# Stage four's first shifted image copies written by VectorE and ScalarE in place of DMAs, five and two unused products on PE ahead of its convolution, and the later image moments moved into its first pass

## What is computed

```
x = x + _L3_conv_ref(_gn(x), ...)

off = conv2d(x, w_off, b_off, (1, 1), 'SAME')              # 3x3, 32 channels in
off = jnp.tanh(group_norm(off, g_gn_off, b_gn_off, K))
upper = jnp.cumsum(y_off[:, CENTER + 1:], axis=1)          # and lower, from the centre outwards
y_coord = jnp.arange(H)[None, None, :, None] + EXT * y_off_new
deformed = jax.vmap(samp)(x, y0i, y1i, x0i, x1i, wy, wx)   # bilinear, here in y alone
out = conv2d(deformed, w_dsc, b_dsc, (K, 1), 'VALID')
out = group_norm(out, g_gn, b_gn, w_dsc.shape[0] // 4)
return jax.nn.relu(out)
```

## Time and profile before

| | |
|---|---|
| median of 3 runs | 1568.82 us (1565.77 to 1573.45) |
| the profiled execution | 1568.02 us, of which the span is 1566.2 us |
| PE, PEld busy | 1358.1 us (87%), 580.5 us (37%) |
| VectorE busy | 1240.1 us (79%) |
| ScalarE busy | 974.9 us (62%) |
| GpSimd busy | 1044.7 us (67%) |
| granted PE clock, mean | 0.939 of full speed |
| stage three's block | about 1074 to 1272 us of the span |
| stage four's block | about 1272 us to the end |

### The profile page before, as it was taken

One profiled execution on the slowest core, in us unless ns is written; L12 is line 12 of the kernel. 1 busy time (PEld: TensorE's weight loads), 2 busy tenths in 40 slices (PEclk: granted clock), 3 DMA queues, 4 the chain that ended last, 5 costly groups with the idle time before them and its releaser, 6 DMA issues. The chain is left out here.

```text
span 1566.2 us, 34078 instructions
## 1 busy us (share of the span) xinstructions
PE 1358.1 (87%) x11812; PEld 580.5 (37%) x11812; DVE 1240.1 (79%) x5001; ACT 974.9 (62%) x1649; POOL 1044.7 (67%) x773
## 2 busy tenths in 40 slices
PE   5999999999999999999995699994887848676775
PEld 1333333333333333333332466661656611121111
DVE  6899999999999999999997455555222258887886
ACT  2688888888888888888883334431000025766654
POOL 4789999999999999999991033233000029998885
PEclk8699999999999999999998899997999978998977
DMA  7000000000000000000000554321000012202001
GB/s 181 9 2 9 4 9 4 2 9 5 9 4 2 9 4 2 12 2 2 1 2 3 125 122 110 84 51 55 2 2 1 2 46 46 46 1 49 11 14 27
DMA packets 24587, 42.31 MB, mean 27 GB/s; under 512 B 8576, under 2 KB 14208, under 8 KB 24416
## 3 DMA queue, kind: packets, MB, share of 16 engines
q1 hardware_dynamic: 21920, 37.64, 10.0%
q10 hardware_dynamic: 2496, 2.50, 0.7%
HBM read 9.20 MB, written 2.10 MB: 7 GB/s over the span
## 5 line engine op out<-in xcount | busy, mean ns | idle before, releaser
L435 POOL TENSOR_SCALAR l_onehot<-l_ib,c_iota 128x512 bf16<-128x512 f16 x250 | 390.0, 1560 | 48.5 <-ACT l_ib L382 48.5
L545 DVE FIND_INDEX8 l_idx<-l_top,l_scored 128x8 uint32<-128x256 f32 x1024 | 413.1, 419 | 0.0
L240 PE MATMUL ps<-l_ct_slot,l_res 32*128 32x512 f32 x2048 | 409.5, 609 | 0.0
L562 DVE CUSTOM_DVE_ANT_0 l_scored<-ps,l_gain 128x256 f32<-128x256 f32 x1024 | 377.8, 416 | 8.4 <-ACT l_gain L364 7.5
L364 ACT ACTIVATE l_gain<-ps 128x768 f32<-128x768 f32 (+1 forms) x384 | 284.2, 740 | 106.6 <-PE ps L240 103.1
L1702 POOL TENSOR_TENSOR l_isum<-l_term 128x512 f32<-128x512 f32 x160 | 204.6, 1307 | 35.5 <-DVE l_term L1806 21.1
L263 PE MATMUL ps<-l_onehot,l_cbp_slot 128*32 128x512 bf16 x3072 | 213.5, 385 | 4.0 <-ACT l_signed L388 2.6
L234 PE MATMUL ps<-l_csq,l_row_slot 32*128 32x512 bf16 x1024 | 154.7, 394 | 12.9 <-DVE l_top L562 6.2
L240 PEld LDWEIGHTS ps<-l_ct_slot,l_res 32*128 32x128 f32 x2048 | 155.8, 193 | 10.7 <-issue 0.8
L1432 PE MATMUL ps<-l_isum,w_l_w_dsc 64*64 64x512 f32 x640 | 104.4, 714 | 59.7 <-POOL l_isum L1702 58.7
L382 ACT CAST l_ib<-ps 128x512 f16<-128x512 f32 x256 | 149.4, 583 | 2.0 <-PE ps L254 2.0
(11 more groups left out here) (178 smaller groups left out, 1935.7 us busy)
## 6 DMA issues: line engine op xcount, KB each, us to landing
l_xi<-l_xt SPq DMA_DIRECT2D x128, 128.0 KB
l_xi<-l_xz SPq DMA_DIRECT2D x36, 144.2 KB, 3.1
X<-in_x SPq DMA_DIRECT2D x16, 128.0 KB, 8.9
l_xr<-l_xt SPq DMA_DIRECT2D x32, 64.0 KB
out<-X SPq DMA_DIRECT2D x16, 128.0 KB, 2.2
l_ct<-in_codes_t SPq DMA_DIRECT2D x4, 448.0 KB, 15.0
l_ct_slot<-l_ct SPq DMA_DIRECT2D x7, 256.0 KB, 2.2
l_cbp_slot<-l_cbp SPq DMA_DIRECT2D x8, 96.0 KB, 1.9
```

What stands on the lines that cost most here:

```text
L240: pe.matmul(ps[:, at + n - FIRST[k], :], res[rows, i, P * tt:P * (tt + 1)], ct_slot[rows, par, :], start=False, stop=True, skip_group_chec ...
L435: nc.gpsimd.tensor_scalar(onehot[:, i % 2, g, 0, :], ib16[:, i % 2, g, :], iota[:, 0:1], None, ALU.is_equal).then_inc(s_near, 1)
L545: nc.vector.max_index(idx8[:, i % 2, n, :], top[:, i % 2, n:n + 1].to_broadcast([P, 8]), scored[:, WIDE * (k % 3) + n - FIRST[k], :]).then ...
L562: nc.vector.tensor_tensor_reduce(out=scored[:, WIDE * (k % 3) + m, :], in0=ps[:, WIDE * (k % 2) + m, :PAIRED], in1=gain[:, WIDE * (k % 2) ...
```

## The change

For quarter 0 the copies in `xi` are no longer sent from `xz`. `xi` is set to zero by GpSimd as a whole, and twelve pieces (g, kx) of each half image are written straight from X by VectorE (four with kx = 0, two with kx = 1) and ScalarE (four with kx = 2, two with kx = 1), normalised on the way. The upper pieces have 17 rows of 32, the lower 15. ScalarE needs `shift` for it, which VectorE now makes in stage three. `xz` of quarter 0 is no longer written. PE multiplies five times into bank 0 once the first four adds are through, and twice more at the head of stage four; nothing reads these products. The moments of quarter 1 stay at the start of stage four, those of quarters 2 and 3 go behind items 4, 6, 8 and 10 of pass 0, with the aggregation behind item 12, the square root at ScalarE's item 11 of pass 1 and the rest behind VectorE's item 13 of pass 1. Names and loops cut:

```diff
+DIRECT = {"dve": [(g, 0) for g in range(G)] + [(0, 1), (1, 1)], "act": [(g, 2) for g in range(G)] + [(2, 1), (3, 1)]}
+PIECE_ROWS = ((0, H // 2 + 1), (H // 2 + 1, H))
+def shifted(xi, g, kx, piece):
+    first, last = PIECE_ROWS[piece]
+    at = (1 + first) * PADW + 1 - kx
+    return xi[C * kx:C * kx + C, g, at:at + (last - first) * PADW].rearrange("p (y x) -> p y x", x=PADW)[:, :, 0:W]
 block_l2, sync:
-            sp.wait_ge(s_next_xz, START + 1)
-            load_columns(sp, xz, xi, 0, range(0, 2), PIECES[0], s_xi[0])
 block_l2, gpsimd:
             nc.gpsimd.memset(xz[:], 0.0).then_inc(s_zero, 1)
+            nc.gpsimd.memset(xi[:], 0.0).then_inc(s_zero, 1)
 block_l2, tensor, at the end:
+            pe.wait_ge(s_out, START + G)
+            for n in range(5):
+                pe.matmul(ps[:, 0, :], ident[:], wt[:].rearrange("p d k m -> p (d k m)")[:, 0:BANK],
+                          start=True, stop=True)
 block_l2, scalar, at the end:
-            act.wait_ge(s_next_xz, START + 1)
-            load_columns(act, xz, xi, 0, range(2, G), PIECES[0], s_xi[1])
+            act.wait_ge(s_next, START + 5)
+            act.wait_ge(s_zero, START + 2)
+            for g, kx in DIRECT["act"]:
+                rows = slice(C * g, C * g + C)
+                nc.scalar.activation(shifted(xi, g, kx, 0), image_rows(X, g, 0), ACT.Identity, bias=xshift[rows, 0:1],
+                                     scale=xrstd[rows, 0:1]).then_inc(s_xi["act"], 1)
 block_l2, vector:
-            nc.vector.tensor_scalar(xz[:, 0, 1:H + 1, 1:W + 1], X[:, 0:HW].rearrange("p (y x) -> p y x", x=W),
-                                    xmv[:, 0, 0:1], xrstd[:, 0:1], ALU.subtract, ALU.mult).then_inc(s_next_xz, 1)
+            nc.vector.scalar_tensor_tensor(out=xshift[:, 0:1], in0=xmv[:, 0:1, 0], scalar=-1.0, in1=xrstd[:, 0:1],
+                                           op0=ALU.mult, op1=ALU.mult).then_inc(s_next, 1)
+            for g, kx in DIRECT["dve"]:
+                rows = slice(C * g, C * g + C)
+                nc.vector.tensor_scalar(shifted(xi, g, kx, 0), image_rows(X, g, 0), xmv[rows, 0, 0:1], xrstd[rows, 0:1],
+                                        ALU.subtract, ALU.mult).then_inc(s_xi["dve"], 1)
 block_l3, sync and scalar:
-            load_columns(sp, xz, xi, 0, range(0, 2), PIECES[1], s_xi[2])
-            load_columns(act, xz, xi, 0, range(2, G), PIECES[1], s_xi[3])
 block_l3, tensor, at the head:
+            for n in range(2):
+                pe.matmul(ps[:, SIDE, :], avg[:, 0, :], sums[:].rearrange("p c m -> p (c m)")[:, 0:BANK],
+                          start=True, stop=True)
 offset_conv:
-                            pe.wait_ge(s_xi[2 * h + e], LOADS // 2)
+                            pe.wait_ge(s_xi[e], (h + 1) * len(DIRECT[e]))
 block_l3, scalar, at the head (the lower pieces as above), then
-            act.wait_ge(s_gn, START + 3 * (J - 1))
-            nc.scalar.activation(std[:, 1:], xmv[:, 1:, 1], ACT.Sqrt, bias=eps[:]).then_inc(s_std, 1)
+            act.wait_ge(s_gn, START + 3)
+            nc.scalar.activation(std[:, 1:2], xmv[:, 1:2, 1], ACT.Sqrt, bias=eps[:]).then_inc(s_std, 1)
 scalar, item 11 of pass 1:
+                                act.wait_ge(s_gn, START + 10)
+                                nc.scalar.activation(std[:, 2:], xmv[:, 2:, 1], ACT.Sqrt,
+                                                     bias=eps[:]).then_inc(s_std, 1)
 block_l3, vector, after the lower pieces and xe:
+            for h in range(2):
+                image_moments(1, h)
+            nc.vector.bn_aggr(xmv[:, 1, :], xstats[:, 1]).then_inc(s_gn, 1)
-            for h in range(2):
-                moments(0, 0, h)
+            moments(0, 0, 0)
+            image_gain(1, 2, 1)
+            moments(0, 0, 1)
 vector, in the passes:
+                    if p == 0 and n in (4, 6, 8, 10):
+                        image_moments(2 + (n - 4) // 4, n // 2 % 2)
+                    if p == 0 and n == 12:
+                        for i in range(2, J):
+                            nc.vector.bn_aggr(xmv[:, i, :], xstats[:, i]).then_inc(s_gn, 1)
+                    if p == 1 and n == 13:
+                        image_gain(2, J, 2)
```

More of the change, by code:

```diff
@@ L1021, with image_rows, load_columns @@
 DIRS = 4
-def load_columns(eng, xz, xi, j, groups, at, done):
+DIRECT = {"dve": [(g, 0) for g in range(G)] + [(0, 1), (1, 1)], "act": [(g, 2) for g in range(G)] + [(2, 1), (3, 1)]}
[4 more added lines that the diff above has]
+    return xi[C * kx:C * kx + C, g, at:at + (last - first) * PADW].rearrange("p (y x) -> p y x", x=PADW)[:, :, 0:W]
+def image_rows(X, g, piece):
+    first, last = PIECE_ROWS[piece]
+    return X[C * g:C * g + C, first * W:last * W].rearrange("p (y x) -> p y x", x=W)
+def load_columns(eng, xz, xi, j, done):
     flat = xz[:, j].rearrange("p y x -> p (y x)")
-    for g in groups:
+    for g in range(G):
         for kx in range(3):
-            eng.dma_start(xi[C * kx:C * kx + C, g, at],
-                          flat[C * g:C * g + C, kx + at.start:kx + at.stop]).then_inc(done, 16)
+            eng.dma_start(xi[C * kx:C * kx + C, g, 0:SHIFTED],
+                          flat[C * g:C * g + C, kx:kx + SHIFTED]).then_inc(done, 16)
 def block_l2(nc, ps, X, io, const, w3, ahead, s_xi):
@@ L1041, in block_l2 @@
     ident, eps = const["ident"], const["eps"]
-    xz, xi, xstats, xmv, xstd, xrstd = (ahead[name] for name in ("xz", "xi", "xstats", "xmv", "std", "rstd"))
+    xz, xi, xstats, xmv, xstd, xrstd, xshift = (ahead[name] for name in ("xz", "xi", "xstats", "xmv", "std", "rstd", "shift"))
     with ExitStack() as ctx:
@@ L1308, in block_l3 @@
     eps = const["eps"]
-    xz, xi, xstats, xmv, std, rstd = (ahead[name] for name in ("xz", "xi", "xstats", "xmv", "std", "rstd"))
+    xz, xi, xstats, xmv, std, rstd, shift = (ahead[name] for name in ("xz", "xi", "xstats", "xmv", "std", "rstd", "shift"))
     with ExitStack() as ctx:
@@ L1995, in build_program @@
                  "xstats": t("l3_xstats", [P, J, 2, 6]), "xmv": t("l3_xmv", [P, J, 2]),
[L1996 to L1997 removed]
+                 "shift": t("l3_shift", [P, J]), "std": t("l3_std", [P, J]), "rstd": t("l3_rstd", [P, J])}
+        s_xi = {name: ctx.enter_context(nc.semaphore("l3_xi_" + name)) for name in ("dve", "act", "dma")}
         block_l2(nc, ps, X, io, const, w3, ahead, s_xi)
```

54 lines of the change are left out of this document (28 added, 26 removed).

## The result

The changed kernel takes 1572.50 us (median of 20 runs, 1566.82 to 1575.97), the kernel before took 1566.92 us beside it (20 runs, 1563.52 to 1573.45). The ratio is 1.0033, with an interval of 1.0022 to 1.0044: slower by 3.4 to 6.9 us, clear of the noise, and still under the 0.5% named ahead. The profiled executions are 1572.16 us after and 1568.02 before, 4.14 apart. What follows accounts for these two; the ratio over all runs, about 5.2 us, is some 1 us more, and that part is not explained.

The account below looks back on a forecast made before the run. It took the chain ending last from stage three's end into stage four as the bound. To the profiled 1568.02 it added 1.05 (convolution's end), 0.2 (pass 0) and 0.26 (pass 1): 1569.5 us, range 1565.0 to 1573.5.

Parts of the forecast that it names:

- The pieces' size: Stage three, upper pieces of 544 elements: 0.53 us each on VectorE, bounds 0.44 and 0.68; six take 3.2.
- VectorE last at the barrier: End of stage three: VectorE arrives last where SP did, and the block ends at 1272.2 in place of 1271.86.
- The five products hidden: Stage three on PE: five unused products at 0.90 us each end at 1268.5, ahead of the barrier.
- The clock down at the barrier: Start of stage four: after 3.7 us of idleness PE's clock is taken to be at half.
- back after 4.1 us: Stage four on PE: full clock returns 4.1 us after the restart; convolution ends at 1281.45, 1.05 us later than before.
- up to 2 us later: Stage four on PE: a clock coming back this much later than before costs 1 us more, 1570.5; counted into the forecast.
- This branch is hidden behind it: Start of stage four: VectorE's and ScalarE's work reaches 1280.8, then waits for PE's convolution until 1281.45.
- Moments in pass 0, +0.2: Pass 0 on VectorE: 3.1 us of moments and aggregations, mostly covered by idleness and GpSimd's work, cost 0.2 us.
- the rival that their cover fails: Pass 0: all 3.1 us of the moved moments count in place of 0.2, giving 1572.4; chance 0.1.
- Pass 1, +0.26: Pass 1: ScalarE's second square root falls where VectorE waits for ScalarE and costs 0.26 us; VectorE's gain costs nothing.
- The clock staying up: Start of stage four: PE's clock does not fall in 3.7 us of idleness; sum 1568.1; chance 0.2.
- Slow pieces: Pieces written across partitions are slow; from 1.19 us each the loss passes 7.8 us, 1575.9 or more; chance 0.04.

Follow-up runs that it names:

- The probe: Changed kernel plus a block behind its last store timing one operation in several shapes; adds some 40 us; VectorE's piece of 17 rows takes 0.83 us.
- the even rows: Changed kernel with pieces cut at 18 and 14 rows in place of 17 and 15; 1568.05 us, ratio 1.0003.
- The kernel with no products: Changed kernel without the seven unused PE products (five in stage three, two in stage four); 1571.78 us, ratio 1.0018.
- eight products: Changed kernel with eight unused PE products in stage three in place of five, and none in stage four; 1573.69 us, ratio 1.0032.
- the moments alone: Kernel before with only the moments of quarters 2 and 3 moved into pass 0, square root and gain into pass 1; 1567.92 us, ratio 0.9998.
- Moments back: Changed kernel with all moments put back at the start of stage four, pieces and products left; 1570.91 us, ratio 1.0007.

## Why the prediction was right or wrong

The class, no change within 0.5%, was right. The time forecast, 1569.5, is 3.0 below the median of 1572.5, and 2.7 below the profiled 1572.16, inside the range. As a forecast of the change it was far off: 1.5 us slower was expected, and 4.1 (profiled) to 5.2 (by the ratio) was measured. The class and the range held because both are wide beside the change; that they held is in good part luck, and does not bear out the working, whose change was a third of the one measured. Point by point:

- **The pieces' size: wrong, and the largest error.** The step was "on the line between them 544 elements take 0.53". It measured 0.83, outside my bounds of 0.44 and 0.68. The line was drawn through 1 element and through 1024 in 32 rows, an even count; the pieces have 17 and 15. Six cost 5.14 in place of 3.2. The block ended 7.69 behind R in place of 6.04 (1272.2 - 1266.16): **+1.65**. The probe and the even rows show the cause: with 18 rows the first instruction behind the barrier came at 6.11, against the 6.04 forecast. The 58 cycles of the Trainium skill's page "VectorE: DVE Perf Modes", section "The TRN2 errata", would have been further off: by them a piece takes an estimated 0.34, and the even piece of 576 elements lasts 0.57.
- **VectorE last at the barrier: right**, by the idle times 0.54, 2.31 and 5.28. ScalarE's piece of 0.725 was also mis-sized (0.84): of the two rows between which I scaled, the one of 512 elements reads PSUM, and from SBUF that size takes 0.81. With VectorE's pieces at their forecast the two would have come about together; with even rows ScalarE ends 0.07 ahead (1268.55 against 1268.62).
- **The five products hidden: right.** Ten rows in 4.56 us are 0.91 a product, against 0.90 taken from the convolution's groups.
- **The clock down at the barrier: right; back after 4.1 us: wrong by 1.6** (5.7), within the "up to 2 us later" that I had named. In after PE was idle for longer than forecast, and the clock stayed full for 4.1 us of it, more than the 3.7 forecast; the kernel with even rows, idle for 3.72 us, shows that the clock can be down after such a time too. PE's work lasted 10.02 us (1273.46 to 1283.48) in place of 9.25: **+0.77**. Together with the barrier the convolution's end is 2.44 later than forecast: 17.73 behind R in place of 15.29.
- **"This branch is hidden behind it": right by 0.33 us only.** The lower pieces of 0.76 and 0.78 in place of 0.49 and 0.66 used up the rest. The kernel with no products shows it.
- **Moments in pass 0, +0.2: they cost nothing** (30.95 against 30.96), and the rival that their cover fails is excluded. After's pass 0 is 0.84 longer, with a stretch at half clock, and as long without the moments in it; why the clock falls there is open. That the moments are free was tried in the kernel before, and eight products agrees.
- **Pass 1, +0.26: nothing** beside it in the moments alone (passes 1 and 2 together 64.46 against 64.44), although the gain took 2.20 us there. The 0.47 of the kernel before was no quiet stretch: that operation ended at 1277.68, GpSimd's at 1277.67. With GpSimd idle the same operation takes 0.16 (at 1265.79 in after). In after the two passes are 1.8 longer; no term of the sum had that, and it is open.
- **The rivals.** The clock staying up did not come about, with PE idle for 5.28 us in place of my 3.7, nor with 3.72 in the kernel with even rows. Slow pieces came, at 0.83 and not beyond 1.19, and for another reason than I had named: the partition shift costs nothing. Its arithmetic, 6(k - 0.53), gives 1.8 at k = 0.83, and the barrier moved by 1.65.
- **The sum.** 1.05 forecast for the convolution's end, 3.50 measured, 3.69 at the first term; 0.46 forecast for the passes, 0.88 measured behind the first term, of which none is shown to belong to the two terms that I had. That last number decides nothing: kernels with the same passes had 274.24 to 276.57 there, with no edit in them to explain it.

## What to carry to other kernels

Before work that was done by DMA is moved to an engine, measure or find a row of the very shape, row count and all, and from the same memory; a line through other shapes of the same operation missed by more than half. Where two branches end within 0.3 us of each other, as here PE's and that of VectorE and ScalarE, a cure of one of them hardly shows, and one ahead of both does (the even rows): cure both in one kernel, then take the parts out again. And a difference of about 1 us behind the edited stretch should be looked up in the clock first, and in a kernel without the edit, before a cause is given to it.

## What the runs showed of the hardware that was not expected

- VectorE's TENSOR_SCALAR in f32: 0.83 us for 17 rows of 32, on 32 partitions as on 128, against 0.535 for 16 rows and 0.57 for 18, both on 32.
- ScalarE's activation: 0.81 us for 512 elements out of SBUF against 0.69 out of PSUM.
- A VectorE operation with two SBUF tiles as inputs, of 1 to 3 elements, lasts until GpSimd ends an instruction, if GpSimd is at work: in all 17 cases in these traces the two ends lie within 0.02 us, and with GpSimd idle it takes 0.16. In the changed kernel's pass 1 it ends at 1348.43 as GpSimd's run ends at 1348.42:

```profile
1343.43 4.99 POOL L1735 TENSOR_TENSOR l_isum<-l_term 128x512 f32<-128x512 f32 x4
...
1346.75 1.68 DVE L1769 SCALAR_TENSOR_TENSOR l_shift<-l_xmv,l_rstd 128x2 f32<-128x2 f32 x1
```

  In the probe it takes 1.17 to 1.20 beside GpSimd's additions of 1.27, while the same product with one tile input takes 0.20. The Trainium skill's page "GPSIMD Engine Reference", section "Specifications", names SBUF interfaces shared with VectorE, and contention with VectorE instructions that have two SBUF inputs or run in a mode with two ports. If one element does not run in such a mode, only the two-input form would wait by that, and the trace agrees.
- PE's clock: idle for 1.30 us, PE came back at full clock; for 2.85 us and more, at half. From the restart the half clock lasted 4.1 us in the kernel before and 5.7 in the changed one. Moments back, with PE's work and idle time ahead of the convolution as in the changed kernel, had 4.0, so PE's own program does not set it; what does is open.
